# Layer 2's finish in a four-layer graph network: negative part on ScalarE, wide splits, and three steps moved into the middle of a quad

## The reference

```python
# --- layer 2 ---
h = relu(layernorm(x)) @ W2
e = leaky_relu(e_src[:, None] + e_dst[None, :], 0.01)
attention = softmax(where(adj > 0, e, -1e12), axis=1)
x = x + elu(attention @ h)
# --- layer 3 ---
h = relu(layernorm(x))
Q, K, V = h @ Wq, h @ Wk, h @ Wv
x = x + softmax(Q @ K.T + mask) @ V
```

## Time and profile before

| | |
|---|---|
| median of 3 runs | 2451.36 us (2449.09 to 2451.63) |
| the profiled execution | 2449.79 us, span 2448.1 us |
| layer 2, loop over g | about 1328 to 1720 us of the span |
| its finish of group 7 | 1720 to 1744 us |
| one group (PE start to PE start) | 54.69, 56.41 or 57.46 us |
| PE busy, whole span | 92% |
| DVE / ACT busy, whole span | 74% / 56% |

### The profile page before, as it was taken

One profiled execution on the slowest core, in us unless ns is written; L12 is line 12 of the kernel. 1 busy time (PEld: TensorE's weight loads), 2 busy tenths in 40 slices (PEclk: granted clock), 3 DMA queues, 4 the chain that ended last, 5 costly groups with the idle time before them and its releaser, 6 DMA issues. The chain is left out here.

```text
span 2448.1 us, 45783 instructions
## 1 busy us (share of the span) xinstructions
PE 2246.1 (92%) x17180; PEld 1704.3 (70%) x17180; DVE 1810.1 (74%) x2893; ACT 1372.0 (56%) x2132; POOL 111.5 (5%) x124
## 2 busy tenths in 40 slices
PE   5899999999999974999978899999699999999998
PEld 4677777867778653888867777777356666666667
DVE  6967879787787843111139999999598988998896
ACT  6655465564655634666645545555355655565556
POOL 2000000010010100000000000000000000000000
PEclk9899999999999986999999999999899999999999
DMA  7544141431411102222211221221211111111000
GB/s 175 108 61 55 42 78 44 78 58 55 78 43 45 35 35 78 86 87 80 88 49 48 73 64 61 68 70 59 74 44 35 44 48 35 44 52 48 27 31 27
DMA packets 63222, 147.77 MB, mean 60 GB/s; under 512 B 10055, under 2 KB 14810, under 8 KB 62045
## 3 DMA queue, kind: packets, MB, share of 16 engines
q1 hardware_dynamic: 56749, 111.62, 14.4%
q0 software_dynamic: 5760, 33.56, 8.3%
q10 hardware_dynamic: 560, 0.52, 0.1%
HBM read 170.82 MB, written 41.96 MB: 87 GB/s over the span
## 5 line engine op out<-in xcount | busy, mean ns | idle before, releaser
L1876 PE MATMUL bank<-VB,ph 128*128 128x257 f16 x2048 | 518.5, 278 | 74.5 <-ACT ph L1756 27.6
L1877 PE MATMUL bank<-VB,ph 128*128 128x257 f16 x2048 | 517.1, 277 | 0.0
L192 PE MATMUL bank<-s_row,kT_hi 128*128 128x512 f16 x1024 | 306.0, 381 | 8.2 <-DMA s_row<-qT_d 6.3
L1387 PE MATMUL bank<-VA,ph 128*128 128x257 f16 x1024 | 280.7, 274 | 7.1 <-DVE VA L1057 7.1
L1880 PE MATMUL bank<-VB,pl 128*128 128x257 f16 x1024 | 286.1, 279 | 0.0
L1876 PEld LDWEIGHTS bank<-VB,ph 128*128 128x128 f16 x2048 | 202.3, 99 | 117.3 <-ACT ag L1777 29.5
L2515 PE MATMUL bank<-VA,ph 128*128 128x257 f16 x1024 | 280.7, 274 | 3.0 <-ACT w_later_hi L2376 2.4
L2517 PE MATMUL bank<-VA,pl 128*128 128x257 f16 x1024 | 280.3, 274 | 0.0
L1389 PE MATMUL bank<-VA,pl 128*128 128x257 f16 x1024 | 280.3, 274 | 0.0
L1388 PE MATMUL bank<-VA,ph 128*128 128x257 f16 x1024 | 280.3, 274 | 0.0
L2516 PE MATMUL bank<-VA,ph 128*128 128x257 f16 x1024 | 280.3, 274 | 0.0
(11 more groups left out here) (333 smaller groups left out, 4596.4 us busy)
## 6 DMA issues: line engine op xcount, KB each, us to landing
mask<-mask_d SPq DMA_DIRECT2D x256, 256.0 KB, 2.7
mask_d<-in_adj POOLq DMA_DIRECT2D x8, 2048.0 KB, 23.3
xg<-x SPq DMA_DIRECT2D x16, 512.0 KB, 4.3
x<-xo POOLq DMA_DIRECT2D x16, 512.0 KB, 2.9
xg<-in_x SPq DMA_DIRECT2D x8, 512.0 KB, 12.9
w_d<-wr SPq DMA_DIRECT2D x8, 512.0 KB, 2.6
f<-w_d SPq DMA_DIRECT2D x8, 512.0 KB, 14.1
x<-xg SPq DMA_DIRECT2D x8, 512.0 KB, 3.9
```

The lines of the kernel that those rows point to most:

```text
L192: last = nc.tensor.matmul(out_ap, st, mv, start=(i == 0), stop=(i == len(todo) - 1))
L1387: nc.tensor.matmul(acc, ph[:, u % HR, c], v_row(V, 0, t), start=(t == 0), stop=False)
L1876: nc.tensor.matmul(acc, p_hi, v_at(V, 0, t), start=first, stop=False)
L1877: last = nc.tensor.matmul(acc, p_hi, v_at(V, 1, t), start=False, stop=final and not weighted)
```

## The change

In layer 2 only: the negative part is taken by ACT (Relu of -ag, placed behind the four `ag`), and exp reads it with scale -1. `kT`, `qT` and `v` are split with one instruction each on ACT and on DVE. Four things move on DVE between the four `p` and the four `pl` of a quad of the next group: inverting the sums (quad 0), the shift `nb` (quad 2), `kT` lo (quad 4, from after quad 3), `qT` lo (quad 6, from after quad 5). `v` lo stays behind quad 7.

```diff
-                        if q == 0 and not isinstance(g, int) and sums_first:
-                            denominators(g - 1)
+                        if not isinstance(g, int):
+                            middle(g - 1, q)
                         for r in range(R):
                             dve.wait_ge(act_q.sem, act_q.at(n, "hi", r))
...
+                    def middle(g, q):
+                        if q == 0:
+                            denominators(g)
+                        if "dve_middle" in work:
+                            work["dve_middle"](dve, g, q)
+
                     def part(dve, g, q):
-                        if q == 0 and (not sums_first or isinstance(g, int)):
-                            denominators(g)
+                        if isinstance(g, int) or not weighted:
+                            middle(g, q)
                         work["dve"](dve, g, q)
...
             def act_part(act, g, q):
+                if q == 0:
+                    act.wait_ge(act_s.sem, act_s.at(g, "ag", R - 1))
+                    nc.scalar.activation(e[:, :], ag[:, :], ACT.Relu, scale=-1.0).then_inc(act_s.sem, act_s.one("below"))
                 if q == 1:
-                    act.wait_ge(dve_s.sem, dve_s.at(g, "mn"))
-                    nc.scalar.activation(e[:, :], e[:, :], ACT.Exp).then_inc(act_s.sem, act_s.one("e"))
+                    act.wait_ge(act_s.sem, act_s.at(g, "below"))
+                    nc.scalar.activation(e[:, :], e[:, :], ACT.Exp, scale=-1.0).then_inc(act_s.sem, act_s.one("e"))
...
                 if q == 7:
-                    for r in range(R):
-                        act.wait_ge(pe_s.sem, pe_s.at(g, "v", r))
-                        hi(v_row(V, 0, g * R + r, D), bank[4 + r][:, 0:D], "v", r)
+                    act.wait_ge(pe_s.sem, pe_s.at(g, "v", R - 1))
+                    hi(own_values(0, g), psum[:, 4:8, 0:D], "v", 0)
+
+            def dve_middle(dve, g, q):
+                if q == 2:
+                    shift(dve, g, nb, mvx, rsx, "nb", "rx")
+                if q == 4:
+                    dve.wait_ge(act_s.sem, act_s.at(g, "hT"))
+                    lo(columns(kT[1], g), psum[:, 4:6, :], columns(kT[0], g), "hT", 0)
+                if q == 6:
+                    dve.wait_ge(act_s.sem, act_s.at(g, "qT"))
+                    lo(qT[:, 1, :, :], psum[:, 4:6, :], qT[:, 0, :, :], "qT", 0)
...
                 if q == 1:
 
                     dve.wait_ge(act_s.sem, act_s.at(g, "ag", R - 1))
-                    nc.vector.tensor_scalar(e[:, :], ag[:, :], 0.0, None, ALU.min
-                                            ).then_inc(dve_s.sem, dve_s.one("mn"))
...
-                if q == 7:
-                    for r in range(R):
-                        dve.wait_ge(act_s.sem, act_s.at(g, "v", r))
-                        lo(v_row(V, 1, g * R + r, D), bank[4 + r][:, 0:D], v_row(V, 0, g * R + r, D), "v", r)
+                if q == 7:
+                    dve.wait_ge(act_s.sem, act_s.at(g, "v"))
+                    lo(own_values(1, g), psum[:, 4:8, 0:D], own_values(0, g), "v", 0)
```

More of the change, by code:

```diff
@@ L1662, in build, with aggregate @@
         Q = T // R
-        def aggregate(V, side, slope=None, wh=None, sums_first=False):
+        def aggregate(V, side, slope=None, wh=None):
             weighted = slope is not None
@@ L2117, in finish_layer2 @@
             pe_s.plan(("hT", K), ("qT", K), ("v", R))
-            act_s.plan(("ag", R), ("e", 1), ("h", R), ("hT", K), ("qT", K), ("v", R))
-            dve_s.plan(("rden", R), ("mn", 1), ("pos", 1), ("x", 1), ("xs", R), ("xm", R), ("xv", 1), ("nb", 1),
-                       ("hT", K), ("qT", K), ("v", R))
+            act_s.plan(("ag", R), ("below", 1), ("e", 1), ("h", R), ("hT", 1), ("qT", 1), ("v", 1))
+            dve_s.plan(("rden", R), ("pos", 1), ("x", 1), ("xs", R), ("xm", R), ("xv", 1), ("nb", 1),
+                       ("hT", 1), ("qT", 1), ("v", 1))
             pool_s.plan(("rx", 1))
@@ L2135, in sums_free, with columns, own_values @@
             def sums_free(act, g):
-                act.wait_ge(dve_s.sem, dve_s.before(g, "pos"))
+                act.wait_ge(dve_s.sem, dve_s.before(g, "x"))
+            def columns(t, g):
+                return t[:, :, ds(g * GW, GW)]
+            def own_values(p, g):
+                at = ds(g * (R * VW) + p * (T * VW), R * VW)
+                return V[:, at].rearrange("p (r w) -> p r w", w=VW)[:, :, 0:D]
             def pool_part(pool, g):
@@ L2142, in pool_part @@
                 nc.gpsimd.dma_start(x3_d[ds(g * P, P), :], xo[:, :]).then_inc(s_xout, 16)
-                pool.wait_ge(dve_s.sem, dve_s.at(g, "qT", K - 1))
+                pool.wait_ge(dve_s.sem, dve_s.at(g, "qT"))
                 pool.sem_inc(s_pass[1], 1)
@@ L2154, in act_part @@
                 if q == 3:
-                    for k in range(K):
-                        act.wait_ge(pe_s.sem, pe_s.at(g, "hT", k))
-                        hi(kT[0][:, k, ds(g * GW, GW)], bank[4 + k][:, :], "hT", k)
+                    act.wait_ge(pe_s.sem, pe_s.at(g, "hT", K - 1))
+                    hi(columns(kT[0], g), psum[:, 4:6, :], "hT", 0)
                 if q == 5:
                     act.wait_ge(s_xout, g * 32 + stores)
-                    for k in range(K):
-                        act.wait_ge(pe_s.sem, pe_s.at(g, "qT", k))
-                        hi(qT[:, 0, k, :], bank[4 + k][:, :], "qT", k)
+                    act.wait_ge(pe_s.sem, pe_s.at(g, "qT", K - 1))
+                    hi(qT[:, 0, :, :], psum[:, 4:6, :], "qT", 0)
                 if q == 7:
-                    for r in range(R):
-                        act.wait_ge(pe_s.sem, pe_s.at(g, "v", r))
-                        hi(v_row(V, 0, g * R + r, D), bank[4 + r][:, 0:D], "v", r)
+                    act.wait_ge(pe_s.sem, pe_s.at(g, "v", R - 1))
[9 more added lines that the diff above has]
+                    lo(qT[:, 1, :, :], psum[:, 4:6, :], qT[:, 0, :, :], "qT", 0)
             def dve_part(dve, g, q):
@@ L2184, in dve_part @@
                             (dve_s.sem, dve_s.at(g, "x")))
[L2185 to L2194, removed]
                 if q == 7:
-                    for r in range(R):
-                        dve.wait_ge(act_s.sem, act_s.at(g, "v", r))
-                        lo(v_row(V, 1, g * R + r, D), bank[4 + r][:, 0:D], v_row(V, 0, g * R + r, D), "v", r)
+                    dve.wait_ge(act_s.sem, act_s.at(g, "v"))
+                    lo(own_values(1, g), psum[:, 4:8, 0:D], own_values(0, g), "v", 0)
             def pe_part(pe, g, q):
                 if q == 2:
-                    pe.wait_ge(dve_s.sem, dve_s.before(g, "v", R - 1))
+                    pe.wait_ge(dve_s.sem, dve_s.before(g, "v"))
                     for k in range(K):
@@ L2208, in pe_part @@
                 if q == 4:
-                    pe.wait_ge(dve_s.sem, dve_s.at(g, "hT", K - 1))
+                    pe.wait_ge(dve_s.sem, dve_s.at(g, "hT"))
                     c = ds(g * GW, GW)
@@ L2215, in pe_part @@
                 if q == 6:
-                    pe.wait_ge(dve_s.sem, dve_s.at(g, "qT", K - 1))
+                    pe.wait_ge(dve_s.sem, dve_s.at(g, "qT"))
                     for r in range(R):
@@ L2223, in finish_layer2 @@
             return {"sync": sync, "pool": pool_part, "act": act_part, "dve": dve_part, "pe": pe_part, "end": end,
-                    "sums_free": sums_free, "V": V}
+                    "sums_free": sums_free, "V": V, "dve_middle": dve_middle}
         def fused_attention():
```

## The result

| | before | changed |
|---|---|---|
| median | 2450.64 us (2448.99 to 2451.63, 5 runs) | 2460.09 us (2459.31 to 2465.24, 5 runs) |
| profiled execution's span | 2448.1 us | 2458.4 us |
| mean granted clock | 0.972 | 0.968 |

The ratio is 1.0044 (95% interval 1.003 to 1.0059): slower by 9.5 us. The forecast was 2460.5 us.

What follows compares the result with a forecast made beforehand. A loop through PE, ACT and DVE via the last `v`, 54.69 us a group, was the bound. Without the clock -0.1, the clock +9.5: 2459.2 us on the profiled execution, stated as 2460.5; range 2444 to 2468.

Steps and rivals of the forecast that it cites:

- The clock: PE behind its wait for quad 2: half-clock stretches in all seven groups, 13.9 us against 4.4 before, so +9.5 us.
- slow stretches: Runs of PE's matmuls with granted clock below 1.00; forecast behind quad 2's wait, 1.67 or 2.76 us each.
- PE's waits: PE idles ahead of quad 0 and of quad 2 in each group: forecast 1.5 and 3.85 us.
- T: The start of quad 0's `p` on DVE, from which the prediction counts times within a group.
- The loop's length: Layer 2's loop per group through PE, ACT and DVE: -1.76 + 1.22 = -0.54 us, so 54.15 us.
- "all of it stays in the stretch": Inverting the sums ahead of quad 0's `pl` leaves its work between T and quad 2; no wait was counted.
- Negative part and shift: Between T and quad 2, DVE loses the minimum (0.61 us) and the wait for POOL (1.15 us).
- cover for the Relu: On ACT, the new Relu (1.06 us) ends at about T + 6.0, before quad 1's first `p` can be rounded.
- The wide splits: One-instruction splits: `v` adds 1.22 us a group between PE's last `v` and T; `kT` and `qT` are covered.
- Tail: Layer 2's end, without quads to hide in: exp's wait for Relu and the wide splits add +3.7 us.
- DVE as the bound: Rival: DVE's own work bounds the group at 49.7 us, so the change gives -31 us, 2420 us; chance 0.08.

Runs made afterwards that it cites:

- Filling the wait: The changed kernel with 14 extra matmuls into an unused bank behind quad 1 of each group, results not read: 2446.35 us, ratio 0.9981.
- `v` narrow: The changed kernel with `v` split in four pieces again, on ACT and on DVE: 2459.67 us, ratio 1.0043.
- `v` early: The changed kernel with `v` made behind quad 5, its hi behind quad 6 on ACT, its lo in the middle of quad 7: 2461.02 us, ratio 1.0039.
- that kernel filled: The kernel before with 10 extra matmuls into an unused bank behind quad 1 of each group, results not read: 2446.93 us, ratio 0.9985.
- late sums and narrow `v`: The changed kernel with sums inverted behind quad 0's four `pl` again and `v` split in four pieces: 2444.83 us, ratio 0.9975.
- late sums alone: The changed kernel with the inverted sums put back behind quad 0's four `pl`: 2447.16 us, ratio 0.9982.
- `v` early and sums late: The changed kernel with `v` made behind quad 5 and the sums inverted behind quad 0's `pl`: 2440.46 us, ratio 0.9956.

## Why the prediction was right, point by point

- **The clock.** Right, and shown: seven slow stretches behind seven long waits. The forecast took two of them to be long and five short, a choice for which it gave no reason; three cost 2.7 or 2.8 us and four 1.5 to 1.7, 14.8 us in all against 13.9. Filling the wait takes 13.7 us away.
- **PE's waits.** 1.25 and 4.08 us against 1.5 and 3.85. The first is shorter because quad 0's `p` starts 0.3 us sooner behind the last `v` than reckoned, so PE's end of quad 7 lies at T + 2.8 and not at T + 2.5; what the first wait lost, the second gained. Quad 0 starts at T + 4.0 as forecast, though not for the forecast reason alone: `ag` and `pl` of quad 0 both stand behind the inverted sums, and with `v` narrow, where ACT's roundings end 0.9 us sooner, the wait is 1.25 us all the same.
- **The loop's length.** 54.04 us (2.48 + 18.87 + 32.69, the last being 1438.40 - 1405.71 of the earlier trace rows) against 54.15. The size was right, the cause half wrong. I charged 1.22 us for the wide `v` as the link that closes the loop. The runs with `v` narrow and with `v` early show that it closes through the sums instead: 1389.78, PE's end of quad 7, to 1405.85 is 16.07 us, plus 37.97 is 54.04. The two loops are 0.2 us apart, and that is luck: it is why the sum came out. The step that failed is "all of it stays in the stretch" for the inverted sums: moving them ahead of `pl` put four `pl` (2.4 us) behind a wait for PE. On the kernel before that alone costs 20 us, about 9 in the loop and 10 through the clock. The trace after shows it only as a wait of 0.22 us.
- **Negative part and shift.** -1.76 us a group. In the kernel before with these alone the group falls from 54.7 to 53.3 us: 1.4. The missing 0.4 is DVE's wait behind the new Relu, which shows in every run with the new Relu ahead of quad 1's roundings and late sums, and in none with early sums; it goes when the Relu moves behind quad 1's roundings. So the prediction's cover for the Relu holds in the changed kernel and not in those. Its account of exp, never late in the loop, agrees with the trace: DVE has no wait there.
- **The wide splits.** `kT` and `qT` are hidden in the loop, as said. `v` costs 0.9 us a group if the sums are late, nothing if they are in the middle. Tail: +3.2 us against +3.7.
- **DVE as the bound.** Refuted: DVE waits 4.76 us for `v` in the changed kernel. With `v` early the wait shrinks to 1.90 us, with `v` narrow DVE is ready 0.9 us sooner, and the group is as long as it was.
- **The total.** 2460.09 us against 2460.5 is closer than the working was: the clock's term was 0.9 us too small, the tail's 0.5 too large, and 0.5 us lie outside both.

## What to carry to other kernels

Look for the loop that a group's critical work closes over all engines, and list every wait of an in-order engine for another along it; when an instruction moves ahead of others, what matters is not its own length but what now stands behind its wait. And where PE idles twice in a group, ask for each of the two waits what a slow stretch behind it would cost. It is free if PE has to wait at its end anyway, as behind quad 0's wait in the kernel before; it costs in full if the loop goes through it. The kernel before was spared in five of seven groups because the slow stretch followed its shorter wait (2.04 to 2.07 us), not the longer one (3.83). Filling a wait with spare matmuls is a cheap test of that, and shortened both kernels.

## What the runs showed of the hardware

- In layer 2's loop, PE's waits of up to 1.9 us were never followed by a lower granted clock in these traces; those of 3.8 us and above always were.
- Between 2 and 3 us it is mixed. Waits of 2.03 to 2.08 us ahead of quad 0 were followed in five of six groups of the kernel before and in six of six of that kernel filled, but in one of six with late sums and narrow `v`, and in one of six with negative part and shift alone. With late sums alone the wait of 2.98 us ahead of one quad 0 was not followed and that of 2.97 ahead of the next was (0.88). Of the 2.4 us waits in the run with `v` early and sums late, four of seven were followed (0.96) and three were not (1.00), with the same work on both sides. What decides between them is not shown. An order whose waits are 2 to 3 us therefore has no fixed time per group.
- In the changed kernel the slow stretches behind waits of 4.08 us cost 1.5 to 1.7 or 2.7 to 2.8 us, in turn from group to group; those behind 5.97 to 5.99 us cost 2.1 to 2.2.
- A copy of 4 x 256 columns out of four banks into strided f16 rows takes 1.01 us on ACT, the subtraction 1.22 us on DVE, as much as into contiguous rows of 1024.
